# Turning the maxima one tile sooner, and issuing three units of transposed scores around k's projection and ahead of v, the logits and the last down projection

## What is computed

```python
xn = _layernorm(x)
x = x + attention(xn) + experts(xn)

# attention
q, k, v = split(xn @ w_in.T + b_in)                 # 16 heads of 8
scores = einsum('bhqd,bhkd->bhqk', q * scale, k) + causal_bias
out = softmax(scores) @ v @ w_out.T + b_out         # nan becomes 0

# experts
scores = softmax(xn @ gate_w.T)
topk_w, topk_i = top_k(scores, 2)
topk_w = topk_w / (topk_w.sum(-1) + 1e-20) * 2.5
combine = zeros(T, 8).at[rows, topk_i].set(topk_w)
g = silu(xn @ w_gate[e]) * (xn @ w_up[e])
y = sum_e combine[:, e] * (g @ w_down[e])
return y + silu(xn @ sw_gate) * (xn @ sw_up) @ sw_down
```

## Time and profile before

| | |
|---|---|
| median of 3 runs | 576.78 us (576.66 to 577.15) |
| the profiled execution's own time | 575.52 us |
| its span | 573.8 us |
| PE, DVE, ACT, POOL busy | 522.2, 452.5, 344.8, 322.3 us |
| mean granted clock of PE | 0.994 of full speed |

### The profile page before, as it was taken

One profiled execution on the slowest core, in us unless ns is written; L12 is line 12 of the kernel. 1 busy time (PEld: TensorE's weight loads), 2 busy tenths in 40 slices (PEclk: granted clock), 3 DMA queues, 4 the chain that ended last, 5 costly groups with the idle time before them and its releaser, 6 DMA issues.

```text
span 573.8 us, 13133 instructions
## 1 busy us (share of the span) xinstructions
PE 522.2 (91%) x4536; PEld 295.5 (51%) x4536; DVE 452.5 (79%) x852; ACT 344.8 (60%) x463; POOL 322.3 (56%) x345
## 2 busy tenths in 40 slices
PE   2679999989999999999999999999999999999985
PEld 1345633656346752576436662466525764366522
DVE  5989798897869968797868968699687978589604
ACT  6422597355963479434983469634794349734693
POOL 2036743775447835479255864478355782558552
PEclk9899999999999999999999999999999999999999
DMA  8984037500475006900268004740069003580001
GB/s 269 267 221 114 12 125 206 132 2 9 146 198 138 2 11 194 261 22 0 104 181 200 0 9 153 220 104 0 22 184 261 18 0 119 164 207 1 10 1 37
DMA packets 45405, 61.99 MB, mean 108 GB/s; under 512 B 4960, under 2 KB 28992, under 8 KB 45376
## 3 DMA queue, kind: packets, MB, share of 16 engines
q1 hardware_dynamic: 42668, 58.37, 36.2%
q10 hardware_dynamic: 2708, 3.24, 1.9%
HBM read 45.21 MB, written 15.34 MB: 106 GB/s over the span
## 4 chain that ended last, share of the span: by engine, by line
PE 60%; DVE 13%; ACT 11%; issue 8%; POOL 5%; DMA 2%; ACTq 1%; POOLq 0%; DVEq 0%
PE banks L673 10%; ACT probs L934 8%; PE banks L537 7%; PE banks L538 6%; PE banks L539 6%; PE banks L573 6%; PE banks L553 6%; PE banks L646 6%; DVE neg_max L1253 5%; PE banks L555 3%; PE banks L554 3%; POOL hid_lo L1024 2%; DVE probs L1229 2%; POOL probs L1044 1%; POOL probs L1016 1%
## 5 line engine op out<-in xcount | busy, mean ns | idle before, releaser
L1253 DVE TENSOR_REDUCE neg_max<-banks 128x2 f32<-128x1024 f32 (+7 forms) x240 | 178.3, 794 | 17.2 <-PE banks L564 16.8
L934 ACT ACTIVATE probs<-banks 128x1024 f32<-128x1024 f32 x160 | 155.4, 1031 | 11.4 <-PE banks L646 9.2
L1044 POOL TENSOR_SCALAR_AFFINE_SELECT probs<-probs 128x512 f32<-128x512 f32 x128 | 90.8, 732 | 124.0 <-ACT probs L934 124.0
L1016 POOL TENSOR_TENSOR probs<-probs,cb 128x512 f32<-128x512 f32 x88 | 113.2, 1286 | 81.4 <-ACT probs L871 80.9
L871 ACT ACTIVATE probs<-banks 128x512 f32<-128x512 f32 (+1 forms) x112 | 67.0, 598 | 134.2 <-PE banks L539 133.9
L1024 POOL TENSOR_TENSOR hid_lo<-probs,hid_hi 128x512 fp32r<-128x512 f32 x85 | 109.6, 1290 | 36.6 <-ACT hid_hi L878 36.3
L1229 DVE TENSOR_TENSOR probs<-probs,banks 128x512 f32<-128x512 f32 (+1 forms) x112 | 76.4, 683 | 35.8 <-POOL probs L1016 27.7
L537 PE MATMUL banks<-x_hi,w_hi 128*128 128x512 f32 (+1 forms) x224 | 95.0, 424 | 4.4 <-DVE probs L1229 4.4
L673 PE MATMUL banks<-probs,v_op 128*32 128x512 f32 (+3 forms) x1024 | 95.2, 444 | 3.7 <-POOL probs L1044 3.5
L538 PE MATMUL banks<-x_lo,w_hi 128*128 128x512 f32 (+1 forms) x224 | 89.0, 398 | 0.0
L539 PE MATMUL banks<-x_hi,w_lo 128*128 128x512 f32 (+1 forms) x224 | 88.8, 396 | 0.0
(11 more groups left out here) (136 smaller groups left out, 552.3 us busy)
## 6 DMA issues: line engine op xcount, KB each, us to landing
cb<-c_dram SPq DMA_DIRECT2D x31, 256.0 KB, 3.9
q_op<-q_dram SPq DMA_DIRECT2D x15, 512.0 KB, 6.8
k_op<-k_dram SPq DMA_DIRECT2D x15, 512.0 KB, 8.2
cb<-c_dram SPq DMA_DIRECT2D x16, 224.0 KB, 4.3
q_dram<-q_parts SPq DMA_DIRECT2D x8, 384.0 KB, 2.5
k_dram<-k_parts SPq DMA_DIRECT2D x8, 384.0 KB, 2.5
cb<-c_dram SPq DMA_DIRECT2D x16, 192.0 KB, 4.2
cb<-c_dram SPq DMA_DIRECT2D x15, 160.0 KB, 4.3
```

Source lines behind the costliest of these rows:

```text
L934: nc.scalar.activation(probs[:, g % 2, 2 * u:2 * u + 2, :], ring[:, at:at + 2, :], ACT.Exp).then_inc(exp_done, 1)
L1016: nc.gpsimd.tensor_tensor(sg[k % 3][:, :], sg[k % 3][:, :], cb[:, tiles_of(b)[k], :], ALU.mult).then_inc(weighted, 1)
L1044: return nc.gpsimd.affine_select(out=view, in_=view, compare_op=ALU.is_ge, fill=0.0, base=0, pattern=[[0, 4], [1, P]], channel_multiplier=-1)
L1253: return nc.vector.tensor_reduce(out, in_, AX.X, ALU.max, negate=True)
```

## The change

`MAXIMA_AT` becomes 11, so that PE turns the maxima in step 11 and ACT copies them behind the silu of tile 11; batch 0 keeps step 12. The turning of x stays in step 12, but goes to step 13 in batch 0. Behind the down projection of tile 11, unit 0, k, and unit 1 stand ahead of the down projection of tile 12, and unit 2 and v with logits ahead of the last down projection. On ACT the copy of k goes behind the first exponential, and the copies of y and q and the router's exponentials each go one unit later; the table load moves from the end of the experts' stage to the head of the attention's. q and the turning of y go one unit later on PE.

```diff
-MAXIMA_AT = NT - 2
+MAXIMA_AT = NT - 3
 MAXIMA_AT_FIRST = NT - 2
+TURN_X_AT = NT - 2
...
                     if k == NT:
+                        scores_t(b, 0, 0)
                         if front:
                             project_k(b + 1)
+                        scores_t(b, 0, 1)
+                    if k == NT + 1:
+                        scores_t(b, 0, 2)
+                        if front:
                             project_v_and_logits(b + 1, vl)
-                        scores_t(b, 0, 0)
-                    if k == NT + 1:
-                        scores_t(b, 0, 1)
                     if k == MAXIMA_AT:
                         transpose_maxima(b)
...
-                    if k == MAXIMA_AT and front:
+                    if k == TURN_X_AT and front:
                         transpose_x(b + 1)
...
-                        if g < GROUPS and (g, u) not in ((0, 0), (0, 1)):
+                        if g < GROUPS and (g, u) not in ((0, 0), (0, 1), (0, 2)):
                             scores_t(i, g, u)
-                        if front and (g, u) == (0, 2):
+                        if front and (g, u) == (0, 3):
                             project_q(i + 1)
-                        if (g, u) == (0, 3):
+                        if (g, u) == (0, 4):
                             transpose_y(i)
...
-                    if k == NT - 1:
-
-                        nc.scalar.activation(table_call[:, :], bqk[:, 1:2], ACT.Exp)
-                    if k == NT - 2:
+                    if k == (MAXIMA_AT_FIRST if i is None else MAXIMA_AT):
                         act.wait_ge(mT_ready, b + 1)
                         nc.scalar.activation(max_rows[:, :], bank_m[0:HALF, :].bitcast(BF16), ACT.Copy
                                              ).then_inc(mrows_done, 1)
+                    if k == NT - 2:
                         high_hidden(b, k - 1)
-                        if front:
-                            take_xT(b + 1)
+                    if front and k == (NT - 1 if i is None else NT - 2):
+                        take_xT(b + 1)
...
             def attend(i, front):
-                if front:
-                    take_k(i + 1)
+                load_exp()
                 for g in range(GROUPS):
                     for u in range(UNITS):
                         n = UNITS * g + u
+                        if front and n == 1:
+                            take_k(i + 1)
...
-                        if (g, u) == (0, 1):
+                        if (g, u) == (0, 2):
                             take_y(i)
                         if front:
-                            if (g, u) == (0, 1):
+                            if (g, u) == (0, 2):
                                 exp_router(i + 1)
-                            if (g, u) == (0, 2):
+                            if (g, u) == (0, 3):
                                 take_q(i + 1)
```

More of the change, by code:

```diff
@@ L741, in first_experts_and_maxima @@
                     if k == NT:
+                        scores_t(0, 0, 0)
                         project_k(1)
+                        scores_t(0, 0, 1)
+                    if k == NT + 1:
+                        scores_t(0, 0, 2)
                         project_v_and_logits(1, vl)
-                        scores_t(0, 0, 0)
-                    if k == NT + 1:
-                        scores_t(0, 0, 1)
                     if k == MAXIMA_AT_FIRST:
@@ L752, in first_experts_and_maxima @@
                         pair(0, None, n + 2)
-                    if k == MAXIMA_AT_FIRST:
+                    if k == NT - 1:
                         transpose_x(1)
@@ L914, in experts, with load_exp @@
                         nc.scalar.activation(o_normT[:, :], nat[:, 0, :], ACT.Copy).then_inc(onT_done, 1)
+            def load_exp():
+                nc.scalar.activation(table_call[:, :], bqk[:, 1:2], ACT.Exp)
             def take_y(i):
```

## The result

The changed kernel takes 584.88 us (median of 4 runs, 584.62 to 585.07), the kernel before 576.79 us beside it (4 runs, 576.66 to 577.15). The ratio is 1.0139, with a 95% interval of 1.0121 to 1.0156: slower by 8.1 us, 1.9 above the 583.0 forecast and inside the range. The profiled execution has a span of 583.3 us and an own time of 585.01.

What follows compares the result with a forecast made beforehand. PE was taken as the bound on average, with about one us of slack in DVE's chain. 6 x 1.0 + 0.2 - 0.1 = 6.1 us on the 576.78 median gave 582.9, say 583.0; range 579.8 to 585.3.

Steps and rivals of the forecast that it cites:

- The maxima: Around tile 10: POOL's low half begins at 270.4, its down projection 0.3 later, PE 0.3 + 0.35 later behind tile 11.
- The lead and its loss: Behind tile 11: first exponential 0.9 sooner, but y's copy waits for the last down and q for v; unit 5 +0.65.
- The chain that is late next: DVE's chain in the attention: starts 2.44 later, PE waits 0.6 at the combine weights, +1.25, less 0.24: +1.0.
- the term of 6 x 1.0: The six like handovers (batches 1 to 6): each 1.0 us slower, bounds 0.65 to 1.4.
- First and last handover: Batch 0's handover +0.2 (0 to 0.5); the last, which prepares no next batch, -0.1 (-0.3 to 0.3).
- DVE's chain gets shorter under fewer masks: Rival: the moved DVE chain meets fewer POOL masks, saving 0.4 or more per handover; 6 x 0.65 + 0.1, 580.8; 18%.
- more: Last rival: the operands' slack goes too, or DVE meets more masks; 1.5 and up per handover, 586; 8%.
- The lead survives: Rival: v with logits ends by 277.9, DVE's slack holds, unit 3's exponential leads by 0.35; 2 us won, 574.8; 8%.

Runs made afterwards that it cites:

- the third place: Changed kernel with maxima back in step 12 and v with logits behind the down projection of tile 12, ahead of unit 2: 578.64 us, ratio 1.0042.
- the second kernel: Changed kernel with v with logits right behind k and maxima back in step 12: 573.06 us, ratio 0.9937; repeated 574.53 us, ratio 0.9963.

## Why the prediction was right

**The maxima: right.** The begin of POOL's low half 270.4, measured 274.99 - 4.52 = 270.47, and it waits for ACT's high half. The down projection waits 0.69 for POOL. Alone, this part costs 0.66 per batch, as summed.

**The lead and its loss: right.** The first exponential was put at 276.1 and is at 275.93; y's copy at 280.35 and is at 280.29; the router's maximum at 279.4 and is at 279.59; q at 281.0 behind a wait of 0.4, and is at 281.26 behind 0.68. Unit 5 is 0.85 later (287.75 - 4.52 - 282.38) and not 0.65.

**The chain that is late next: right in mechanism.** The combine weights were to end at 292.45 and end at 296.89 + 0.19 - 4.52 = 292.56. PE waits 0.46 for them, where I had 0.6, and turns them 1.37 later, where I had 1.25.

**Mis-sized: the outputs, and with them the term of 6 x 1.0.** I wrote "The outputs are copied at 293.30 + 2.2, so they are there at 296.2; PE comes for them at 295.20 + 1.0 = 296.2, with no further wait." From the combine weights to the copy of the outputs lay 3.25 us before (290.05 to 293.30), 3.66 after (296.89 to 300.55). I had let DVE's work keep its length. The normalisation in between took 1.76 instead of 1.15, under POOL's masks. So PE waits 0.55 and starts 301.29 - 4.52 - 295.20 = 1.57 later. The term measured 1.58 in this handover and 1.29 to 1.60 in five of the six, 0.61 in the sixth, which has no normalisation ahead of the outputs: 7.9 in all, and not 6.0. Moving the normalisation away gave back 3.3 us. In the first two of the five, at 1.29, DVE took 12.65 and 12.56 us from the router's maximum to the end of the combine weights, and not 12.97 as here. No run left the masks out, so that they are the cause of the slow rows rests on where the rows lie: in the traces of the kernel before, the changed one, the one with v at the third place and the one with one more reduction, every slow cast and subtraction of k and q lies under a mask, and none that is free of one is slow.

**First and last handover: small, as said, but at the edge of their bounds.** The first attention costs some 0.5 of its own (the upper bound; the term was 0.2), after the clock's 1.4 to 1.5 is taken out. The last is -0.35 (the term -0.1), just outside the bound of -0.3.

**The sum.** 7.9 + 0.5 - 0.35 = 8.1, where I had 6.1. The direction and the cause were forecast; the size was not: the six measured 1.32 each on average, just inside the upper bound of 1.4, and three of them lie above it. That the range still holds the time owes something to luck.

**The rivals.** That DVE's chain gets shorter under fewer masks was wrong for this change: it lost 13.28 - 12.97 = 0.3 us up to the combine weights, which is the wait for q that it no longer has, and then got longer. With v right behind k and in the kernels with work added, the chain did get shorter by some 0.6. The Trainium skill (SBUF — State Buffer, Who interferes with whom) says that a DVE instruction in a two-port mode, which a tensor_scalar can enter, and a GpSimd instruction lock each other out of a shared port. This fits the rows of the normalisation, 1.15 us between the masks and 1.76 under them. Which way a move goes is decided by where the masks come to lie. I had given the way to a shorter chain 18%, and with the longer one I reckoned only in the last rival. The rival "more" named the right cause with too high a price. "The lead survives" needs v to end by 277.9, and the kernels with v ahead show what it is worth. In the kernel before's time, v ends at 277.5 right behind k and at 277.9 behind unit 1 (maxima in step 12), and both kernels are faster; at the third place it ends at 278.7, and the kernel is slower.

Not separated is what the three early units bring by themselves. They are in the kernel with v ahead and the maxima back, together with the new places on ACT, and its gain over before is 2.0 to 3.8 us in two trials. Of the profiles that start alike, those of the kernel before (573.8) and of this one with the normalisation late (571.5) are 2.3 apart.

## What to carry to other kernels

An engine that shows no wait and no waiter can still have a chain with about one us of slack: measure it as the distance from each result's end to its use, and price a delay of its head against that. Put the producer of another engine's long chain ahead of work that only fills PE, and the early scores behind it. And where the late chain shares time with an engine that slows it, don't carry its durations over to the new place, but bound them by the slow and the fast rows of the same operation. Look at the granted clock before a loss is put down to a wait: a longer wait of PE can be followed by a stretch at the lower level, which costs extra.

## What was not expected of the hardware

**The clock of PE at the start has two outcomes.** Windows 24 to 34 and 34 to 42 us (length, busy time and count of PE, PEld, DVE, ACT and POOL, granted clock, DMA's busy share, GB/s), of the kernel before and then of the changed one:

```profile
24.00:34.00 10.00, 7.15 (x18) 4.37 (x18) 8.47 (x10) 4.12 (x6) 1.27 (x1) 0.67 0.66 181
34.00:42.00 8.00, 7.00 (x74) 4.23 (x74) 7.73 (x12) 2.13 (x4) 3.62 (x3) 1.00 1.02 268
```

```profile
24.00:34.00 10.00, 6.29 (x18) 3.83 (x18) 8.99 (x11) 4.02 (x6) 1.27 (x1) 0.83 0.66 177
34.00:42.00 8.00, 6.95 (x59) 4.47 (x59) 5.53 (x8) 1.45 (x3) 2.51 (x2) 0.79 0.98 260
```

What PE did is in its timelines, before and then after:

```profile
34.81 0.41 PE L573 MATMUL banks<-k_op,q_op 64*64 64x512 bf16 x4 [2.42 <-DMA k_op<-k_dram]
...
35.51 0.40 PE L538 MATMUL banks<-x_lo,w_hi 128*128 128x512 f32 x1
```

```profile
34.85 0.41 PE L574 MATMUL banks<-k_op,q_op 64*64 64x512 bf16 x4 [3.11 <-DMA k_op<-k_dram]
...
35.81 0.63 PE L539 MATMUL banks<-x_lo,w_hi 128*128 128x512 f32 x1
```

In the kernel before PE gets its upper level (2.4 GHz) late, has an idle time of 2.42 us and keeps the level (1.00). In the changed one it gets it sooner (0.83), stands idle 3.11 us, and falls to the lower level (1.2 GHz) for some 3 us (0.79): the same matmul takes 0.63 and not 0.40. That costs some 1.5 us in the one profile. It isn't the change's doing: the change touches nothing that runs in the first 42 us, and the profiles of the second kernel and of the same with the normalisation late have equal periods and the two different starts (0.83 and 0.79, 0.69 and 1.00), and spans of 572.9 and 571.5. The runs of one kernel spread by two us and more (before: 575.0 to 577.7); that the start makes this spread isn't shown, as only the profiled runs have a trace. In either case 1.0 us between the medians of two such kernels is not an effect.

**What a mask costs DVE at the same instruction.** Four normalisations take 1.15 or 1.76 us, a cast 0.41 to 0.43 or 0.74 to 0.85, a subtraction 0.69 or 1.00, all in this handover and with nothing changed but the time. Not every row under a mask is slow: in the kernel before, 12 of the 16 first subtractions of k and q overlap one and take 0.69. Over the whole program the normalisation's 32 instructions take 10.4 us in the kernel before and 13.6 in the changed one.
